# Magnitudes of three chunks of an eight-bit layer written during the attention before it

## The reference

```python
x = x + jnp.tanh(g_xattn[1]) * _L1_xattn_ref(_layernorm(x, axis=-1), ctx_512, ctx_512, ...)   # second attention, 16 heads
x = x + jnp.tanh(g_ffn[1]) * _L1_ffn_ref(_layernorm(x, axis=-1), ...)                         # eight-bit linear layer

def quant_fp8(x):
    amax = jnp.max(jnp.abs(x)).astype(jnp.float32)
    scale = jnp.minimum(FP8_MAX / jnp.maximum(amax, 1e-12), FP8_MAX)
    x_fp8 = jnp.clip(x * scale, -FP8_MAX, FP8_MAX).astype(jnp.float8_e4m3fn)
    return (x_fp8, 1.0 / scale)
# _L1_ffn_ref
w_fp8, w_scale = quant_fp8(weight)
x_fp8, x_scale = quant_fp8(x2d)
acc = jnp.matmul(x_fp8.astype(jnp.float32), w_fp8.astype(jnp.float32).T)
out2d = (acc * (x_scale * w_scale) + bias).astype(jnp.bfloat16)
```

## Time and profile before

| | us |
|---|---|
| median of three runs | 371.13 |
| lowest and highest of them | 368.69, 371.86 |
| the profiled execution, its own time | 367.93 |
| its span, first to last instruction | 365.9 |
| granted TensorE clock over the span | 0.979 of full speed |

### The profile page before, as it was taken

One profiled execution on the slowest core, in us unless ns is written; L12 is line 12 of the kernel. 1 busy time (PEld: TensorE's weight loads), 2 busy tenths in 40 slices (PEclk: granted clock), 3 DMA queues, 4 the chain that ended last, 5 costly groups with the idle time before them and its releaser, 6 DMA issues.

```text
span 365.9 us, 8956 instructions
## 1 busy us (share of the span) xinstructions
PE 338.1 (92%) x2890; PEld 267.0 (73%) x2891; DVE 253.4 (69%) x690; ACT 232.6 (64%) x471; POOL 161.5 (44%) x211
## 2 busy tenths in 40 slices
PE   4999969888999999999999998879999999999995
PEld 2768846557899999999999973656666666666774
DVE  1479998925665655654545567878888988777696
ACT  1489958136566666665666533576678678665586
POOL 7088996199655555556556344311132132101000
PEclk9999998859999999999999999999999999999998
DMA  6999963021222222232233115112011000000005
GB/s 181 323 403 423 426 240 115 2 58 31 87 74 79 79 73 72 72 81 77 72 78 80 43 59 184 61 59 60 3 60 59 2 2 2 3 2 3 0 30 201
DMA packets 15338, 36.21 MB, mean 99 GB/s; under 512 B 3526, under 2 KB 6748, under 8 KB 13772
## 3 DMA queue, kind: packets, MB, share of 16 engines
q1 hardware_dynamic: 10508, 24.66, 18.4%
q0 software_dynamic: 3936, 10.48, 10.2%
q10 hardware_dynamic: 864, 0.66, 0.5%
HBM read 22.28 MB, written 13.52 MB: 98 GB/s over the span
## 4 chain that ended last, share of the span: by engine, by line
PE 76%; DVE 10%; ACT 5%; DMA 3%; POOL 2%; issue 2%; SPq 0%; DVEq 0%; ACTq 0%
PE two L1999 15%; PE two L1984 15%; PE two L2141 5%; PE two L2018 5%; PE two L2171 4%; PE two L2206 4%; PE two L2127 4%; PE two L2107 3%; PE two L2009 2%; PE two L2198 2%; DMA x_sb<-in_x 2%; DVE stat L1109 1%; PE two L1866 1%; PE two L2187 1%; DVE x_sb L1191 1%
## 5 line engine op out<-in xcount | busy, mean ns | idle before, releaser
L1398 DVE SCALAR_TENSOR_TENSOR gate<-th,two 128x512 f32<-128x512 f32 x39 | 26.8, 688 | 58.0 <-ACT th L869 32.6
L613 POOL DMA_INDIRECT y_d<-y_sb,goal_i x39 | 38.5, 987 | 48.6 <-ACT y_sb L879 48.3
L607 POOL DMA_INDIRECT xg<-xn_d,slot_i x39 | 37.9, 973 | 21.3 <-DVE slot_i L1343 10.4
L1984 PE MATMUL two<-wh,gh 128*128 x156 | 44.1, 283 | 0.2 <-issue 0.2
L636 POOL TENSOR_TENSOR rstd<-var,half 128x2 f32<-128x2 f32 x14 | 9.9, 706 | 76.9 <-DVE var L1463 76.9
L1984 PE MATMUL two<-wh,gl 128*128 x156 | 43.8, 281 | 0.0
L1984 PE MATMUL two<-wl,gh 128*128 x156 | 43.8, 281 | 0.0
L858 ACT ACTIVATE xq<-xg 128x256 f32<-128x256 f32 x39 | 23.5, 603 | 30.8 <-DMA xg<-xn_d,slot_i 30.2
L869 ACT ACTIVATE th<-two 128x512 f32<-128x512 f32 x39 | 23.3, 596 | 27.3 <-PE two L1999 17.4
L573 POOL TENSOR_TENSOR wl<-wl,wh 128x512 fp32r<-128x512 f32 x32 | 40.2, 1278 | 0.1
L1496 DVE TENSOR_REDUCE nm<-two 128x8 f32<-128x960 f32 x32 | 36.1, 1152 | 4.5 <-PE two L2127 4.1
(11 more groups left out here) (307 smaller groups left out, 857.6 us busy)
## 6 DMA issues: line engine op xcount, KB each, us to landing
wl<-in_wmoe SPq DMA_DIRECT2D x8, 1024.0 KB, 12.1
y_d<-wh SPq DMA_DIRECT2D x4, 1024.0 KB
yg<-y_d SPq DMA_DIRECT2D x7, 512.0 KB, 3.6
xn_d<-x_sb SPq DMA_DIRECT2D x8, 258.0 KB, 5.9
x_sb<-in_x SPq DMA_DIRECT2D x8, 256.0 KB, 6.0
out_x<-of SPq DMA_DIRECT2D x8, 256.0 KB, 2.0
xg<-xn_d,slot_i POOLq DMA_INDIRECT x39
y_d<-y_sb,goal_i POOLq DMA_INDIRECT x39
```

Source lines behind the costliest of these rows:

```text
L607: pool.indirect_dma_start(xg[:, n % 2, :], None, xn_d, bass.IndirectOffsetOnAxis(ap=slot_i[:, n:n + 1], axis=0)).then_inc(gathered[n % 2], 16)
L613: pool.indirect_dma_start(y_d, bass.IndirectOffsetOnAxis(ap=goal_i[:, n:n + 1], axis=0), y_sb[:, n % 2, :], None).then_inc(y_stored[n % 2] ...
L1398: dve.scalar_tensor_tensor(gate[:, k, :], th[:], 1.0, bank[2 + k][:], ALU.add, ALU.mult).then_inc(gate_ok, 1)
L1984: ins = pe.matmul(bank[6 + k][:, 0:D], (gl if part == 2 else gh)[:, k, a], (wl if part == 1 else wh)[:, bass.ds(e + (C * FF + c * D), D)], ...
```

## The change

Three things are edited. A new buffer `size_sb` holds magnitudes of chunks 0, 1 and 2. In `norm3(b)` with `b` below 3, ScalarE writes them with two Abs instructions of 128x256, ahead of the two that write `xn_sb`. In the eight-bit layer ScalarE's first three `scaled_up` are gone, and VectorE has a new function `magnitudes` for chunks 0 to 2 that scales, floors and rounds to 16 bits in one operation; it runs ahead of the three small operations for the bias. On TensorE the first two turns stand ahead of the wait for the bias operand.

```diff
+        MADE_WHOLE = 3
+        size_sb = sb("size_sb", [P, MADE_WHOLE * U * D])
             def norm3(b):
                 act.wait_ge(rstd3_ok, b + 1)
+                if b < MADE_WHOLE:
+                    for u in range(U):
+                        nc.scalar.activation(size_sb[:, cols(2 * b + u, D)], x_tile(2 * b + u), ACT.Abs,
+                                             scale=rstd3[:, b % 2, u:u + 1], bias=less3[:, b % 2, u:u + 1])
                 for u in range(U):
                     ins = nc.scalar.activation(xn_sb[:, cols(2 * b + u, D)], x_tile(2 * b + u), ACT.Identity, scale=rstd3[:, b % 2, u:u + 1],
                                                bias=less3[:, b % 2, u:u + 1])
...
             act.wait_ge(scale_ok, 1)
-            scaled_up(0)
-            scaled_up(1)
-            scaled_up(2)
             scaled_up(3)
             copy_y8T(0)
...
             then(dve.tensor_scalar(red[:, 6:7], red[:, 4:5], FP8_MAX, FP8_MAX, ALU.mult, ALU.min))
+            dve.wait_ge(scale_ok, 1)
 
             def floored(b):
 
-                dve.wait_ge(ym_ok, b + 1)
+                dve.wait_ge(ym_ok, b + 1 - MADE_WHOLE)
                 dve.tensor_scalar(ym[:, b % 4, :], ym[:, b % 4, :], LEAST, None, ALU.max).then_inc(yf_ok, 1)
+
+            def magnitudes(b):
+
+                dve.tensor_scalar(ym[:, b % 4, :], size_sb[:, cols(b, U * D)], red[:, 12:13], LEAST, ALU.mult,
+                                  ALU.max).then_inc(yf_ok, 1)
...
+            magnitudes(0)
+            push(0)
+            magnitudes(1)
+            push(1)
             then(dve.tensor_scalar(sxp[:], ones[:], red[0:3, 6:7], None, ALU.mult))
             then(dve.tensor_copy(sxh[:], sxp[:]))
             dve.scalar_tensor_tensor(sxn[0:3, :], sxh[:].bitcast(F32), ident[0:3, 2:3], sxp[:], ALU.mult,
                                      ALU.subtract).then_inc(sxn_ok, 1)
-            floored(0)
-            push(0)
-            floored(1)
+            magnitudes(2)
             own.mark(dve.reciprocal(red[:, 8:9], red[:, 6:7]))
-            push(1)
+            push(2)
             own.settle()
             dve.tensor_scalar(red[:, 13:14], red[:, 8:9], red[:, 9:10], None, ALU.mult).then_inc(scale2_ok, 1)
-            floored(2)
-            push(2)
             floored(3)
...
+            turn(0)
+            turn(1)
             pe.wait_ge(sxn_ok, 1)
             bias_of(0)
+            linear(0)
             bias_of(1)
-            turn(0)
-            turn(1)
-            linear(0)
             turn(2)
             bias_of(2)
             linear(1)
```

## The result

| | before | changed |
|---|---|---|
| median of 22 runs each, us | 369.75 | 371.52 |
| lowest to highest, us | 366.38 to 371.86 | 369.01 to 375.32 |
| profiled execution, span, us | 365.9 | 370.5 |

The ratio is 1.0049, with a 95% interval of 1.0025 to 1.0073: about 1.8 us (0.9 to 2.7) slower. The highest run of the changed kernel, 375.32 us, was in a slower state (over 1.5% above the fastest run of the same kernel), and the ratio leaves it out. The two single spans differ by 4.6 us; where that comes from has to be read first.

The account below looks back on a forecast made before the run. TensorE was taken to bound the kernel (76% of the span on the last-ending chain). Three passes, +2.79 us, and the eight-bit layer, -0.29, make +2.50 on a median of 371.13: 373.6 us, range 370.4 to 376.0.

Parts of the forecast that it names:

- the price of a pass is 0.98 - 0.05 = 0.93 us: Second attention, three passes: two Abs delay the maxima TensorE loads by 0.98 us, less 0.05 slack; 2.79 us in all.
- rival c: Attention: each pass pays twice, as TensorE also waits for VectorE's maxima; 376.4 us, chance 0.06.
- rival a: Attention: the new instructions are hidden in ScalarE's idle time, leaving only the tail's gain; 370.8 or 370.5 us, chance 0.10.
- 0.66 us earlier: Eight-bit layer: the first turn starts right behind TensorE's filling matmuls, at 349.54 in place of 350.20.
- +0.18 us: Eight-bit layer: VectorE's last push comes later by this net, +0.63 for longer operations less waits of 0.26 and 0.19.
- a last turn that waits for yt: Eight-bit layer: sign of being right, TensorE's last turn waiting for VectorE's output, leaving the end 0.29 us earlier.
- 0.29 predicted: Eight-bit layer: the end comes 0.29 us earlier, since VectorE's late last push takes part of the first turn's 0.66.
- rival (b): Eight-bit layer: VectorE's magnitudes takes 0.69 us an operation, not 0.48; 374.3 us, chance 0.10.
- +2.50: Whole kernel: 2.79 us later from the passes less 0.29 us from the eight-bit layer, 0.68% more.
- On their median it makes 371.13 + 2.50: Whole kernel: the sum added to the median of the three runs shown, giving 373.6 us.
- The profiled execution's 367.93: Whole kernel: span of the profiled execution before the change, noted as below the three runs shown; plus the sum, 370.43.

Follow-up runs that it names:

- e1: The kernel before plus only the buffer and the two Abs in three passes, output unread; ratio 1.0091, passes 14.30 us.
- e7: The changed kernel run again, unaltered, against runs of the kernel before on the same chip; ratio 1.0089 (1.0053 to 1.0125).
- e4: The kernel before with only TensorE's order changed (two turns ahead of the bias, linear(0) ahead of the second bias); one run, 371.56 us, tail 15.46 us.
- e0: The kernel before with the buffer size_sb added and never used; ratio 1.0020 (0.9985 to 1.0056).
- e3: The changed kernel with one Abs of 128x512 behind the pass's last exponential in place of the two in norm3; ratio 1.0007, passes 13.37 us.
- the six runs: Runs of the kernel before plus each of the two Abs done twice in three passes, output unread; ratio 1.0235, passes 16.8 us.

## Why the prediction was right and wrong

**The three passes: right.** The step "the price of a pass is 0.98 - 0.05 = 0.93 us" is the measured 14.30 - 13.37, three times, in the changed kernel, in e1 and in e7. No pass paid twice (rival c) and nothing was hidden (rival a). The row that decided it was the pair of weight loads with an equal distance in a pass without normalisation: it tells slack from waiting, which a share of busy time can't.

**The first turn: right in kind, too large.** I had it begin at once behind the filling, 0.66 us earlier. It came 0.47 us earlier, in e4 too. The load of its weights, first in the changed kernel and then before:

```profile
354.45 0.14 PEld L2332 LDWEIGHTS two<-ident,yt 128*128 128x128 f32 x1
```

```profile
349.97 0.14 PEld L2323 LDWEIGHTS two<-ident,yt 128*128 128x128 f32 x1
```

It begins behind the last filling matmul's load, at 354.45, and the turn begins 0.22 us later. In the kernel before that step is as long (349.97 to 350.20), but the two bias matmuls ran over it. I had put it at nothing.

**VectorE's queue: the working was wrong.** I wrote that it is "+0.18 us" later at the last push. It was 0.08 us earlier (10.71 us behind the mark, before 358.29 - 347.50 = 10.79). I had found two waits that go and missed the third: before, the floors of chunks 6 and 7 took 0.72 us since ScalarE wrote ym of chunk 7 only until 356.73, and they now take 0.49. The rows of the kernel before, ScalarE's and VectorE's:

```profile
355.98 0.75 ACT L1059 ACTIVATE ym<-xn_sb,red 128x512 bf16<-128x512 f32 x1
```

```profile
356.33 0.72 DVE L1667 TENSOR_SCALAR ym<-ym 128x512 bf16<-128x512 bf16 x2
```

So VectorE doesn't set the last turn, which comes 0.46 us earlier and not 0.29; the sign that I had named, a last turn that waits for yt, didn't come. VectorE takes part of the gain back behind it, through the sum that ScalarE's rescale waits for 0.15 us, a wait that wasn't in my sum. The end is 0.28 us earlier against 0.29 predicted. The two errors cancelled by luck, and that number is no proof of its working. Magnitudes itself took 0.49 us against 0.48, so rival (b) is out.

**The sum: +2.50 against 3 x 0.93 - 0.28 = +2.51 us** by the traces (2.45 by the spans from the first oT). As 0.68% it lies within both intervals; weighted by the inverse squares of their widths the two ratios give 1.0061.

**The predicted time, 373.6 us: too high by 2.1.** The step that failed is "On their median it makes 371.13 + 2.50". The median of three runs was above the kernel's own: 22 runs give 369.75, and the runs of before in the later comparisons 368.6 to 369.8. With it, 1.4 us of the miss is the base, and 0.7 is that this comparison's 1.8 us lies below the 2.5. Against the real median a forecast of 373.6 says 1.04% slower, over twice the 0.49% measured, though the working said 0.68. The profiled execution's 367.93 was a warning that I noted and then set aside. The trace shows what scatters, too: everything ahead of the first oT, by 5 us, while the 115.8 us behind it are the same in the traces of before and of e0.

## What to carry to other kernels

Slack is a property of one place in a queue, not of an engine's share: 3.2 us of idle time in a pass didn't hide 0.98 us ahead of the piece that the bound engine wanted next, and the same magnitudes made behind the last exponentials of the pass (e3) cost nothing. When two edits come together, run each by itself: here a reordering on TensorE alone held all the gain in the traces, and the part that needed a buffer and six more ScalarE instructions in the attention gave only loss. For a change of a few tenths of a per cent, add it to a base of many runs, and compare passes of one trace rather than times of single executions.

## What the runs showed that I had not expected

A wait of TensorE in the middle of a busy stage had a second price here. Waits of 0.86 and 1.36 us a pass left the granted clock at 1.00 in all passes traced. A wait of 1.84 us was followed, in all three passes of that kernel's trace, by a stretch of some 3.4 us (estimated from the windows) at the lower level of the clock, which cost 1.6 us more. Filling the wait with four useless matmuls (1.9 us of them) gave that back, 16.8 to 15.28 us a pass. Where between 1.36 and 1.84 us it sets in wasn't tried, nor whether the length of the wait alone decides.

How often the clock falls is open. Three passes as in the trace, 3.45 us longer each, would be a ratio of 1.028, and with no fall of the clock it would be 1.0155; the six runs give 1.0235 (1.0193 to 1.0277), between the two. They range from 375.99 to 381.27 us with mean clocks of 0.966 to 0.982, the profiled one being the slowest. That would fit a clock that falls in some of the passes of each run, but only one of the six was traced.
